# Reordering TensorE between the LoRA stage and the gate/up stage of a two-layer decoder

## What is computed

```python
x = layernorm(x + L0_ffn(x))      # W, a bias and a LoRA of the rank that a gate picks for each row
# fourth sublayer, its attention first
q = x @ Wq.T + (x @ Aq.T) @ Bq.T  # k and v in the same way
attn = (q + k + v) / 3.0
o = attn @ Wo.T + (attn @ Ao.T) @ Bo.T
x1 = x + o
g, u = lin_lora(x1, gate), lin_lora(x1, up)   # 1792 columns each
x = layernorm(x1 + lin_lora(silu(g) * u, down))
```

## Time and profile before

| | |
|---|---|
| median of 3 runs | 661.95 us (659.49 to 662.01) |
| the profiled execution | 661.55 us, of which 659.7 us from its first to its last instruction |
| mean granted TensorE clock | 0.996 of full speed |
| TensorE busy | 642.2 us (97%) |
| VectorE, ScalarE busy | 394.1 us (60%), 384.2 us (58%) |
| DMA, mean over the span | 97 GB/s |
| the stretch of the change | about 161 to 242 us |

### The profile page before, as it was taken

The page is one execution under the profiler, slowest core; times in us unless marked ns, Lnnn a source line. Parts: engine busy times, 40 slices in busy tenths (PEclk is TensorE's granted clock), DMA queues, the critical chain, the costliest instruction groups (busy, mean ns, idle before and its releaser), DMA issues.

```text
span 659.7 us, 8518 instructions
## 1 busy us (share of the span) xinstructions
PE 642.2 (97%) x3232; PEld 473.7 (72%) x3232; DVE 394.1 (60%) x622; ACT 384.2 (58%) x528; POOL 67.5 (10%) x117
## 2 busy tenths in 40 slices
PE   9999999999999999999999999999999999999995
PEld 6655455554547778888888888886777888888874
DVE  2778867749688859676766527324675221215566
ACT  3877778866787777766767236213456333226532
POOL 1122213302231000000000000001111000000012
PEclk9999989999999999999999999999999999999999
DMA  6870287522323324332421003038000222100002
GB/s 226 294 269 33 85 267 192 160 80 64 100 99 108 103 70 141 102 108 77 126 79 31 1 0 129 1 113 365 0 5 29 80 97 67 61 1 0 1 32 97
DMA packets 25015, 64.19 MB, mean 97 GB/s; under 512 B 5478, under 2 KB 10022, under 8 KB 24079
## 3 DMA queue, kind: packets, MB, share of 16 engines
q1 hardware_dynamic: 23486, 61.50, 28.9%
q10 hardware_dynamic: 1488, 2.15, 1.0%
HBM read 58.90 MB, written 4.73 MB: 96 GB/s over the span
## 4 chain that ended last, share of the span: by engine, by line
PE 88%; DVE 4%; ACT 4%; issue 2%; POOL 1%; POOLq 0%; ACTq 0%; DVEq 0%
PE bank L1004 19%; PE bank L1083 8%; PE bank L1082 8%; PE bank L991 7%; PE bank L992 7%; PE bank L993 7%; PE bank L766 4%; PE bank L843 4%; PE bank L597 3%; PE bank L716 2%; PE bank L679 1%; PE bank L690 1%; PE bank L631 1%; PE bank L622 1%; PE bank L751 1%
## 5 line engine op out<-in xcount | busy, mean ns | idle before, releaser
L1191 ACT ACTIVATE line<-line 128x1024 f32<-128x1024 f32 x87 | 91.2, 1049 | 0.1
L991 PE MATMUL bank<-xh,wh 128*128 128x512 f32 x224 | 87.5, 391 | 0.0
L992 PE MATMUL bank<-xl,wh 128*128 128x512 f32 x224 | 87.4, 390 | 0.0
L993 PE MATMUL bank<-xh,wl 128*128 128x512 f32 x224 | 87.3, 390 | 0.0
L1004 PE MATMUL bank<-wh,xh 128*128 128x512 f32 x192 | 76.0, 396 | 0.2 <-DVE xl L2082 0.2
L1004 PE MATMUL bank<-wh,xl 128*128 128x512 f32 x192 | 74.9, 390 | 0.0
L2165 DVE SCALAR_TENSOR_TENSOR arena<-bank,ff_s,arena 128x512 f32<-128x512 f32 x28 | 21.0, 751 | 72.9 <-PE bank L1083 63.7
L2082 DVE TENSOR_TENSOR xl<-arena,xh 128x1024 fp32r<-128x1024 f32 (+1 forms) x26 | 29.6, 1141 | 35.2 <-ACT xh L1508 35.0
L1082 PE MATMUL bank<-xh,wh 128*128 128x512 f32 x128 | 50.2, 392 | 0.0
L1083 PE MATMUL bank<-xl,wh 128*128 128x512 f32 x128 | 49.9, 390 | 0.0
L1508 ACT ACTIVATE xh<-arena 128x1024 fp32r<-128x1024 f32 (+1 forms) x26 | 25.6, 991 | 41.3 <-PE bank L1004 34.8
(11 more groups left out here) (211 smaller groups left out, 1276.2 us busy)
## 6 DMA issues: line engine op xcount, KB each, us to landing
codes<-in_c_gu SPq DMA_DIRECT2D x14, 512.0 KB, 3.6
scales<-in_s_gu SPq DMA_DIRECT2D x28, 256.0 KB, 3.8
codes<-in_t_gu SPq DMA_DIRECT2D x8, 512.0 KB, 4.2
codes<-in_c_dn SPq DMA_DIRECT2D x7, 512.0 KB, 5.1
scales<-in_s_dn SPq DMA_DIRECT2D x14, 256.0 KB, 4.0
fold<-in_t_dn SPq DMA_DIRECT2D x1, 3584.0 KB, 16.6
scales<-in_t_gu SPq DMA_DIRECT2D x6, 512.0 KB, 3.7
x<-in_x SPq DMA_DIRECT2D x2, 1024.0 KB, 6.0
```

The lines of the kernel that those rows point to most:

```text
L991: pe.matmul(dst, wh[:, s, c:c + P], xh[:, k, cols], start=(k == 0), stop=False)
L992: pe.matmul(dst, wh[:, s, c:c + P], xl[:, k, cols], start=False, stop=False)
L993: last = pe.matmul(dst, wl[:, s, c:c + P], xh[:, k, cols], start=False, stop=(k == KD - 1))
L1191: nc.scalar.activation(below(slot), below(slot), ACT.Prelu, bias=bias, scale=scale, alpha=alpha).then_inc(bent, 1)
```

## The change

Only TensorE's order changes, and the banks of the x1 transposes; no instruction is added or taken away, and VectorE, ScalarE, GpSimd and SyncE keep their order.

```diff
+X1_BANK = (7, 4, 5, 6)
...
                     attention_lora(n)
+                if FIRST_M <= t < FIRST_M + KD:
+                    attention_product(t - FIRST_M)
                 if t + 2 < NT - 1:
                     ffn_W(t + 2)
                 elif t == NT - 1:
                     ffn_W(t)
-                if FIRST_M <= t < FIRST_M + KD:
-                    attention_product(t - FIRST_M)
+                    attention_out(0)
                 if t + 2 < NT:
                     ranks(t + 2)
                 lora_out(t)
                 if t >= 2:
                     x_T(2, t - 2)
             for t in range(2):
-                attention_out(t)
+                attention_out(1 + t)
                 x_T(2, NT - 2 + t)
...
                 if b == 0:
-                    pe.wait_ge(xt_ready, 3 * NT)
+                    pe.wait_ge(ln_sum, 3 * NT - 2)
+                elif b == 3:
                     pe.wait_ge(xl_ready, NT)
-                elif b == 1:
-                    pe.wait_ge(ln_sum, 3 * NT - 2)
-                else:
-                    pe.wait_ge(xl_ready, NT + b - 1)
-                transpose_tile(b, rbuf[:, b % 2, :], bank[6 + b % 2])
-
-            for t in range(2, NT):
+                elif b >= 4:
+                    pe.wait_ge(xl_ready, NT + b - 3)
+                transpose_tile(b, rbuf[:, b % 2, :], bank[X1_BANK[b % 4]])
+
+            for t in range(3, NT):
+                x1_T(t - 3)
                 attention_out(t)
-                if t < NT - 1:
-                    x1_T(t - 2)
                 if t == KD:
                     gu_lora(0)
-                elif t == NT - 2:
-                    x1_T(t - 1)
+            x1_T(NT - 3)
             gu_lora(1)
             for b in range(NT - 2, NT):
                 x1_T(b)
...
-                x_T_out(3 * NT + b, 6 + b % 2, xh)
+                x_T_out(3 * NT + b, X1_BANK[b % 4], xh)
...
-                x_low(3 * NT + b, 6 + b % 2)
+                x_low(3 * NT + b, X1_BANK[b % 4])
```

## The result

| | before | changed kernel |
|---|---|---|
| median | 661.4 us (659.49 to 662.1, 9 runs) | 663.89 us (661.23 to 665.35, 9 runs) |
| ratio | | 1.0046, 95% interval 1.0031 to 1.006 |
| profiled execution | 661.55 us, span 659.7, clock 0.996 | 665.35 us, span 663.5, clock 0.991 |

By the ratio the change costs 3.0 us: 0.5%, against a forecast of 3.1. The two profiled executions lie 3.8 us apart, 0.7 us beyond the forecast; where these are is part of what follows.

The account below looks back on a forecast made before the run. TensorE, busy 97% of the span, was taken as the bound, through its idle time and clock. 3.1 - 0.8 - 0.8 = +1.4, plus 1.7 for the clock, made +3.1 on 661.55: 664.6 us, range 661.3 to 666.2.

Parts of the forecast that it names:

- Part 1: Pieces of M ahead of W: in turn 3 TensorE waits for VectorE's sums, cost 3.1 us; with turn 4, shift 2.3.
- Turn 4: W of block 6 no longer waits for VectorE's sum of block 3, the second piece of M covering it: gain 0.8 us.
- Part 2: attention_out(0) ahead of the last LoRA output: TensorE saves 2.1 us of its own waits, VectorE and ScalarE get nothing.
- Part 3: x1's transposes ahead, in four banks: VectorE's wait for block 7's high part at 228.35 goes, gain 0.8 us.
- The two new short waits of TensorE: In the x1 transposes, TensorE waits on ScalarE's copies of x1: 0.7 and 0.5 us.
- The wait before gu_lora(2): Ahead of gate/up, TensorE's wait of 0.31 us for VectorE's low part grows to 2.1 us, spending TensorE's own savings.
- Part 4: TensorE's clock falls behind the new 3.1 us wait, in products of M and W from 165 to 170: 1.7 us lost.
- Sum: Whole kernel: +1.4 us without the clock, +1.7 for the clock, +3.1 us in all, giving 664.6 us.
- A: Rival: the clock holds behind the new wait, so only +1.4 us, 662.9 us; chance 0.26.
- B: Rival: ScalarE's copy of block 7 comes the full 2.3 us later, second gain gone: +4.0, 665.5 us; chance 0.12.
- C: Rival: faster, VectorE makes the two sums by 162.3 so no new wait: 659.9 or 657.6 us; chance 0.06.
- D: Rival: x1 transposes in four banks bring nothing to those who wait; inside the forecast at a price of 0.

Follow-up runs that it names:

- e1: Changed kernel with only the first piece of M put back behind W of block 5: ratio 0.9964, 659.09 us median.
- e5: Kernel before with only attention_out(0) moved ahead of the last LoRA output; x1 transposes, their banks and the pieces of M as before: ratio 1.0002.
- e6: e1 with tile 2's LoRA operand made earlier, by ScalarE's copy ahead of its second rounding and VectorE's low part ahead of the second low weights: ratio 0.9971.
- e7: e6 with ScalarE's first dequantising steps of tile 2 also ahead of its second rounding: ratio 0.9927, 656.26 us median.
- e4: Changed kernel with three extra matmuls, results overwritten, filling TensorE's wait before the first piece of M: ratio 1.0018, 662.11 us median.
- e3: Changed kernel with all pieces of M back behind the W products, leaving attention_out(0) ahead and the x1 transposes ahead over four banks: ratio 0.9996.
- e2: Kernel before with only the four pieces of M moved ahead of the W products; attention_out(0), x1 transposes and banks as before: ratio 1.0048.

## Why the prediction was right, step by step

- **Part 1.** The wait: 3.1 forecast, 4.17 us from the LoRA parts' start to the piece of M against 1.06 to W, so 3.1 measured; e1 removes it. TensorE came 0.06 us behind the sums, as forecast. Turn 4: 0.8 forecast, 1.03 measured (fifth lora_T +4.80, sixth +3.77). The term was under-sized by 0.2. W of block 6 could have been issued 0.11 us behind lora_T, as the piece of M is now, and stood 1.04 behind it: 0.93 and not 0.84. And behind a wait it took 3.70 us, without one 3.60:

```profile
176.80 0.27 PE L848 MATMUL bank<-ident,early_w 128*64 128x128 f32 x1
176.91 3.60 PE L874 MATMUL bank<-arena 128*128 128x512 f32 x8
...
180.56 3.60 PE L844 MATMUL bank<-arena 128*128 128x512 f32 x8
184.00 1.04 PE L834 MATMUL bank<-arena 128*128 128x112 f32 x8
```

- **Part 2.** The waits went, and VectorE and ScalarE got next to nothing of them: 0.31 us by e5, where nothing was forecast.
- **Part 3.** 0.8 forecast, 1.03 to 1.09 measured for the whole x1 part; the 0.31 of part 2 is in it. The path is the one forecast: block 7's copy, which was to be delayed 1.5 us less than the rest, starts at 229.86, 2.30 us later than before (the 0.32 us taken off) against a shift of 3.77. The term is short by a stop of VectorE of 0.2 us that I overlooked, three rows ahead of the one counted. Its low part started 0.81 us behind the instruction ahead of it before, and 0.60 in the changed kernel (before, then changed):

```profile
224.36 0.69 DVE L1948 TENSOR_TENSOR x<-x,rbuf 128x512 f32<-128x512 f32 x1
225.17 0.69 DVE L1779 TENSOR_TENSOR xl<-bank,xh 128x512 fp32r<-128x512 f32 x1
```

```profile
228.49 0.68 DVE L1947 TENSOR_TENSOR x<-x,rbuf 128x512 f32<-128x512 f32 x1
229.09 0.68 DVE L1778 TENSOR_TENSOR xl<-bank,xh 128x512 fp32r<-128x512 f32 x1
```

  The two new short waits of TensorE were 0.34 and 0.30 us, where 0.7 and 0.5 were forecast. The wait before gu_lora(2): 2.1 forecast, 2.02 measured. VectorE's low part of the operand ends at 244.02, or 243.7 with the 0.32 us of the later start taken off; 244.0 was forecast with the lower clock. That the start hangs on ScalarE and VectorE is shown by e6 and e7.
- **Part 4.** Price and place of the clock's fall: 1.7 forecast, 4.80 - 3.1 = 1.7 measured, and e4 shows that it was the wait's. What the forecast lacks is the same step at the wait before gu_lora(2), which I had put at 2.1 us myself: longer than the 2.0 us of one-column products, and so by my own argument a place for a fall. It costs 0.85 us where it occurs. That argument was thin besides: the stretch ahead of the fall at 84.46 is busy throughout by the earlier trace rows, no run tests whether the one-column products brought it about, and of the nine traces, whose code is the same there, four have it and five do not.
- **Sum.** 3.1 - 1.03 + 1.7 - 1.03 + 0.85 = 3.6 at gu_lora(3), 3.47 at the end of the profiled execution. Against 3.1 that is 0.37 less for the two under-sized gains (1.03 and 1.03 against the unrounded 0.84 and 0.85) and 0.85 more for the forgotten fall; they offset each other in part, and that the ratio's 3.0 us meets the forecast to 0.1 is luck to that extent. The ratio's 3.0 us is below the trace, and the mean clocks go with that: of the nine runs of the changed kernel four at mean clock 0.991 took 665.0 to 665.4 us and a fifth 663.75, the three at 0.993 or 0.994 663.6 to 663.9, the one at 0.995 661.2. All but the fifth of the shorter runs had less of the lower clock; which of the falls they lacked, the two behind the waits or the early one of the earlier trace rows, a mean cannot tell.
- **Rivals.** A (the clock holds) is what e4 imitates: 0.87 us later at the end of its trace, where A had 1.4. The run of 661.2 us may be such a case, which is not shown, since it has no trace. B's extra delay did not occur (block 7's copy, part 3), C's missing wait neither. D falls by e5.

## What to carry to other kernels

Before a product is moved ahead of another, ask what the other one was hiding: a reader put directly behind the producer of its operands pays the whole latency of the engine between, and here 3.5 us of W had covered it. Waits that vanish from the busiest engine are worth something only where its partners come earlier too; follow the partners' chain to the next place where the busy engine needs them, and put the slack there in order first. Price a new wait of TensorE with the clock that may fall behind it.

## What the runs showed of the hardware

Behind waits of the same length the clock fell in some executions and not in others. Behind the 3.0 us of turn 3 it fell in both traces that have the wait. Behind the 2.0 us before gu_lora(2) it fell in the changed kernel and in e3, and not in e1 and e4, nor behind the 2.34 us in e6. In e2 it fell at 201.94, behind the waits of 0.84 and 0.42 us that are in the kernel before as well, where the clock held; so my statement that idle times up to 1.07 us leave it alone holds for that one execution only.

```profile
198.50:201.94 3.44, 2.17 (x9) 1.00 0.00 0
201.94:205.35 3.41, 3.41 (x10) 0.50 0.57 147
```

A fall costs what the waits behind it leave: 1.7 us in turn 3, where nothing absorbs it, 0.85 behind gu_lora(2), and in e2 0.5 (3.77 at the eighth lora_T and 4.26 at gu_lora(2)), where the wait of 0.86 us before x_T(2, 6) went in exchange. Each fall ahead of the last microseconds of an execution lasted 3.4 us.
